# One Trainium2 core, last layer: sixteen shared tiles before the slots, returned rows added at the end, the last router begun inside the attention

## The chip, the cores and the metric

The kernel runs on one of the eight cores of one Trainium2 chip (trn2). A core has TensorE (PE), VectorE (DVE), ScalarE (ACT), GpSimd (POOL) and a queue engine SyncE (SP), each with its own instruction stream; they meet only at semaphores. The metric is the device time of one execution in microseconds; lower is better.

## What is computed

The input `x` is 16 sequences of 128 rows of 256 float32. Four layers follow one another; each adds a gated attention and a gated feed-forward step to `x`. Only the last of each is touched by the change:

```python
x = x + tanh(g_xattn[3]) * L3_xattn(layernorm(x), ctx)   # 16 heads, keys from ctx
x = x + tanh(g_ffn[3]) * L3_ffn(layernorm(x))
# L3_ffn: 7 routed experts of which each row takes 2, and one shared expert for all
gate = xt @ Wr + br                     # 7 logits a row
_, ids = top_k(gate + gate_bias, 2)
probs = softmax(gate where chosen, else -inf)
u = xt @ Wup[e] + bup[e]
g = silu(u @ Wgate[e] + bgate[e]) * u
out = sum_e probs[e] * (g @ Wdown[e] + bdown[e])
out = out + shared expert of the same form, unweighted
```

## The kernel before

`x` stays in on-chip memory as 16 tiles `x[:, t, :]` of 128 rows by 256. All order is written out by hand, one program for each engine; every engine works strictly in the order of its own program. The names that matter:

**The third attention in the code, `attention(3)`.** It runs over the tiles t = 0..15. TensorE computes the scores (`scores(t, c, u)`, two halves c, L1766) into PSUM banks 0 to 3, DVE takes row maxima (L1225) and subtracts them (L1231), ACT exponentiates (L836) with the factor `q_rms`, TensorE turns the result round (`turn`, L1776), ACT copies it out (L842), TensorE multiplies by the values (`values`, L1787) and ACT copies the result (L853). TensorE turns the rows (`turn_rows`, L1799), DVE divides (`denominators`, `norm`, L1238 and L1245), TensorE turns once more (`turn_out`, L1805), ACT copies (`o_evac`, L847), and TensorE applies the output projection (`project_out`, L1811); DVE adds it to `x` (`add_out`, L1133, semaphore `resid6`) and takes mean and variance of the tile (`tile_stats`, L1125 and L1129). POOL makes the reciprocal root from the variance (`deviations(7)`, L584 and L587). The last tile has nothing after it that could fill the waits of this chain. At the front of this attention DVE scales the sums of squares of the queries (`q_var`, L1616), POOL takes the power -1/2 of it (`q_rms`, L803), and only then ACT can exponentiate.

**The router, `router(7, ...)`.** For each tile DVE writes the normalised rows into `xs3` (`norm_rows`, L1529, in the trace as `late`, since that is the buffer), TensorE turns them (`turn_x`, L2048), ACT copies the result into `xt_all` (`route_in`, L989), and TensorE multiplies by the router's weights, 7 columns (L2056). `turn_x` for tile t+2 follows the logits of tile t. After each four tiles DVE chooses two experts per row (`choose`, from L1652 on to L1488), TensorE counts with triangular matrices which place each row gets in its expert (`slots`, L2030 to L2034), and DVE reads that (`place`, L1499 to L1503).

**Sending.** POOL scatters the rows to their places in HBM with indirect DMAs, 32 of them, 128 rows each (`send`, L605), in eight groups of four with a small copy ahead of each (L601). Then SP loads the places back in blocks of 128 rows, called slots (38 of them, `N3`, into a ring of six tiles, L550).

**The expert loop.** The work list is `work3(i)`, i = 0..53: before, i = 0..11 are shared-expert tiles 0 to 11 (`NS3 = 12`), i = 12..49 the 38 slots, i = 50..53 the shared tiles 12 to 15. Each item is a chain: TensorE up and gate in one fused product (`up3`, L2208), DVE adds the bias (`sums`, L1625), ACT Silu (L1089), DVE product (`hidden`, L1631), TensorE turns (`turn_h`, L2216), ACT copies (L1094), TensorE down (`down3`, L2230). TensorE's program for step i is: turn slot i+1 (`turn_slot`, L2091), up of i, down of i-2, turn of i-1. The result of a shared tile is added to `x` (`add_shared`, L1641); that of a slot gets its bias (`out_slot`, L1637) and POOL scatters it to `y_rows` in HBM (`send_back`, L646).

**The end.** SP waits for all scatters, loads the rows back in token order (`yc`, eight loads of 512 KB, L560, four groups `g` of four tiles), and DVE adds them with their weights (`returned(g)`, eight instructions for each group, L1686). Before, `returned(0)` stands in DVE's program at i = 52, ahead of the sums of item 53, and groups 1 to 3 after the loop. SP stores each group of `x` when it is finished (L563).

## Time and profile before

| | us |
|---|---|
| median of 3 runs (lowest, highest) | 897.07 (896.79, 898.49) |
| the profiled execution's own time | 894.69 |
| its span, first to last instruction | 892.9 |

The profile is of one execution. Busy shares over the whole span: PE 84%, DVE 66%, ACT 46%, POOL 40%. The mean granted TensorE clock is 0.915 of full speed. The time outside the span is 894.69 - 892.9 = 1.8 us. In a timeline a row is one instruction or a run of the same one; the bracket at its end is how long the engine was idle before it and what ended that. "x8" counts instructions as the chip ran them (a float32 matmul is two).

### The profile page before, as it was taken

The numbers are of one execution on the slowest core, as the hardware profiler recorded it, in microseconds if no ns is written. First come the engines' busy times: TensorE is split into PE (matmuls) and PEld (weight loads), VectorE is DVE, ScalarE is ACT, GpSimd is POOL, SyncE is SP. The second block draws the span as 40 slices with busy tenths as digits, with TensorE's granted clock in tenths as the row PEclk, the third lists the DMA queues.
The fourth block names the chain that finished last, engine by engine and source line by source line (L and its number), as shares of the span: only waits on it lengthen the run. The fifth ranks groups of instructions, "written<-read, shape, count | busy, mean of one in ns | idle before, by whom it ended". The sixth has DMA issues, their size and how long they took to land.

```text
span 892.9 us, 15919 instructions
## 1 busy us (share of the span) xinstructions
PE 754.0 (84%) x4531; PEld 499.4 (56%) x4539; DVE 586.8 (66%) x1356; ACT 415.2 (46%) x904; POOL 354.8 (40%) x588
## 2 busy tenths in 40 slices
PE   3999795998774289899999968999988889999982
PEld 2455453554342156686888657566657556666651
DVE  5799697677775967873322375788865765445446
ACT  3466465676572014331477554666762132333320
POOL 5000453355447633347377564111131761343320
PEclk9999898999998579959999989999995899999995
DMA  6354308999206891144455352000003222222226
GB/s 209 121 163 144 98 12 274 308 292 313 60 0 252 327 303 45 69 169 159 132 154 155 107 191 76 21 20 21 12 17 132 97 88 80 86 87 86 66 85 213
DMA packets 90652, 117.00 MB, mean 131 GB/s; under 512 B 12438, under 2 KB 81209, under 8 KB 89291
## 3 DMA queue, kind: packets, MB, share of 16 engines
q1 hardware_dynamic: 83802, 99.15, 36.7%
q0 software_dynamic: 6768, 16.86, 5.3%
q8 instruction: 40, 0.66, 0.3%
q14 instruction: 42, 0.34, 0.1%
HBM read 55.04 MB, written 58.43 MB: 127 GB/s over the span
## 4 chain that ended last, share of the span: by engine, by line
PE 50%; DVE 12%; SPq 9%; POOL 9%; issue 9%; ACT 7%; DMA 3%; DVEq 0%; POOLq 0%; ACTq 0%
PE ps L2208 8%; SPq L401 7%; POOL x_rows L605 6%; PE ps L1776 4%; PE ps L2230 4%; PE ps L2098 4%; PE ps L1766 3%; ACT work L836 2%; ACT probs_t L842 2%; PE ps L1973 2%; PE ps L2116 2%; PE ps L1811 2%; PE ps L2091 2%; PE ps L2173 2%; PE ps L1864 2%
## 5 line engine op out<-in xcount | busy, mean ns | idle before, releaser
L842 ACT ACTIVATE probs_t<-ps 128x1024 f32<-128x1024 f32 x64 | 65.5, 1024 | 68.8 <-PE ps L1776 68.8
L1225 DVE TENSOR_REDUCE row_max<-ps 128x8 f32<-128x1024 f32 x64 | 77.5, 1211 | 12.1 <-PE ps L1766 11.8
L1089 ACT ACTIVATE ctx_cols<-ctx_cols 128x256 f32<-128x256 f32 x54 | 22.5, 417 | 123.9 <-DVE ctx_cols L1625 123.9
L1625 DVE TENSOR_TENSOR ctx_cols<-ps,ctx_rows 128x512 f32<-128x512 f32 x54 | 37.3, 691 | 62.3 <-PE ps L2208 62.2
L1231 DVE TENSOR_TENSOR work<-ps,row_max 128x1024 f32<-128x1024 f32 x64 | 76.9, 1202 | 1.2
L1776 PE MATMUL ps<-ident,work 128*128 128x128 f32 x512 | 70.7, 282 | 3.8 <-ACT work L836 2.7
L2208 PE MATMUL ps<-early,xt 128*128 x152 | 71.5, 593 | 0.0
L646 POOL DMA_INDIRECT y_rows<-ctx_cols,w2d x38 | 37.6, 990 | 78.5 <-DMA y_rows<-ctx_cols,w2d 47.1
L2230 PE MATMUL ps<-early,ctx_cols 128*128 (+1 forms) x216 | 57.9, 392 | 11.8 <-ACT ctx_cols L1094 11.8
L1776 PEld LDWEIGHTS ps<-ident,work 128*128 128x128 f32 x512 | 57.3, 143 | 18.4 <-ACT work L836 13.2
L2230 PEld LDWEIGHTS ps<-early,ctx_cols 128*128 128x128 f32 x216 | 41.9, 196 | 41.3 <-issue 23.7
L1787 PEld LDWEIGHTS ps<-probs_t,work 128*32 128x32 f32 x1024 | 24.3, 110 | 52.0 <-ACT probs_t L842 46.7
L587 POOL TENSOR_TENSOR rstd<-var_eps,consts 128x2 f32<-128x2 f32 (+1 forms) x64 | 47.4, 740 | 10.2 <-POOL var_eps L584 5.4
L646 POOL DMA_INDIRECT y_rows<-wgb,probs_t x39 | 38.3, 983 | 22.2 <-issue 16.0
L1787 PE MATMUL ps<-probs_t,work 128*32 128x128 f32 x1024 | 41.7, 281 | 5.4 <-ACT probs_t L842 5.4
L1544 DVE SCALAR_TENSOR_TENSOR xn<-ps,work,xn 128x128 f32<-128x128 f32 x39 | 13.7, 351 | 48.6 <-ACT xn L1021 48.6
L584 POOL TENSOR_TENSOR var_eps<-mv,consts 128x2 f32<-128x2 f32 x64 | 15.0, 235 | 72.6 <-DVE xn L1117 33.2
L2098 PE MATMUL ps<-late,xt 128*128 x156 | 40.1, 380 | 0.0
L669 POOL COPY work<-ctx_rows 128x256 f32<-128x256 f32 x16 | 6.3, 398 | 84.0 <-PE ps L1787 84.0
L1125 DVE BATCH_NORM_STATS2 st<-x 128x6 f32<-128x256 f32 x96 | 35.8, 415 | 4.9 <-POOL x L737 0.9
L1766 PE MATMUL ps<-early,xt_all 64*128 64x512 f32 x128 | 38.5, 679 | 0.0
L1766 PE MATMUL ps<-late,xt_all 64*128 64x512 f32 x128 | 36.7, 651 | 1.9 <-DVE work L1231 1.9
(326 smaller groups left out, 1887.5 us busy)
## 6 DMA issues: line engine op xcount, KB each, us to landing
x_rows<-pad_row SPq DMA_DIRECT2D x1, 17415.0 KB, 68.5
work<-x_rows SPq DMA_DIRECT2D x77, 129.0 KB, 2.1
x_rows<-pad_row SPq DMA_DIRECT2D x1, 7740.0 KB, 35.8
x_rows<-pad_row SPq DMA_DIRECT2D x1, 7611.0 KB, 94.1
early<-in_w3st SPq DMA_DIRECT2D x8, 512.0 KB, 6.4
work<-y_rows SPq DMA_DIRECT2D x16, 256.0 KB, 3.0
early<-y_rows SPq DMA_DIRECT2D x8, 512.0 KB, 7.4
late<-in_w2u SPq DMA_DIRECT2D x1, 2304.0 KB, 8.5
```

The source lines that it names most:

```text
L401: sp.dma_start(kz[HD * h:HD * (h + 1), t % KR, :, h % 4, :], ctx_cols[HD * h:HD * (h + 1), t, :, :]).then_inc(sem(f"att.k{t % KR}"), 16)
L605: pool.indirect_dma_start(out=rows, out_offset=bass.IndirectOffsetOnAxis(ap=pos[:, k, t:t + 1], axis=0), in_=xs[:, t, :], in_offset=None). ...
L646: pool.indirect_dma_start(out=rows, out_offset=bass.IndirectOffsetOnAxis(ap=dest[:, i % 8:i % 8 + 1], axis=0), in_=y[:, i % 4, :], in_offs ...
L842: act.activation(probs_t[:, :, :], ps[:, 4:6, :], ACT.Copy).then_inc(sem("att.evac"), 1)
L1225: dve.tensor_reduce(row_max[:, u, 8 * c:8 * c + 8], scores(c), AX.X, ALU.max).then_inc(sem("att.max"), 1)
L1231: dve.tensor_tensor(probs[:, u, c, :].rearrange("p (h k) -> p h k", k=P), scores(c), row_max[:, u, 8 * c:8 * c + 8].unsqueeze(2).to_broadc ...
L1766: op = mm(bank(2 * c + b), cols(xt_all, t)[64 * b:64 * b + 64, c, :], kz[64 * b:64 * b + 64, t % KR, c, :, :].rearrange("p h k -> p (h k)" ...
L1776: op = pe.transpose(ps[:, 4 + k // 4, (k % 4) * P:(k % 4 + 1) * P], probs[:, u, c, k * P:(k + 1) * P], ident[:, :])
L1787: op = mm(ps[32 * g:32 * g + HV, 6, (2 * c + b) * P:(2 * c + b + 1) * P], vaug[:, u, 8 * c + k, :], probs_t[:, b, g * P:(g + 1) * P], star ...
L2098: op = mm(bank(i % 2, 2 * HID), xti[:, j, :], w2u[:, j, e].rearrange("p w n -> p (w n)"), start=(j == 0), stop=(j == 1))
L2208: op = mm(bank(i % 2), xti[:, j, :], w13[:, e, j, :], start=(j == 0), stop=(j == 1))
L2230: op = mm(bank(4 + i % 2, D), ht3[:, i % 2, j, :], wd3[:, e, j, :], start=(j == 0), stop=(j == 1))
```

## The change

Five edits, all at the last layer:

- `NS3` goes from 12 to 16: all shared tiles stand ahead of the 38 slots, none behind.
- `returned(0)` leaves the loop; all four groups are added after it.
- The router of the last layer is split. TensorE turns tiles 0 and 1 after its last `turn` of the attention, and does the logits of tiles 0 to 7 (`last_logits`, two tiles at a time, each with the turn of the tile two further) at four places between the last tile's steps. Tiles 8 to 15 follow after the attention, with the same `slots` calls, each later by a few tiles. Turned tiles go through banks 2 and 3 instead of 6 and 7, and the logits of the last two groups into banks 6 and 7 (`LB3`), because banks 0 to 3 are free once the scores are.
- DVE normalises rows 0 to 3 and 4 to 11 inside the attention's end, and chooses the experts of group 0 (`choose_last(0)`) ahead of the last `add_out`; the setup of `run3` stands ahead of the attention. POOL makes the roots of tiles 0 to 11 between its steps of the attention (`dev7`).
- At the attention's front DVE does the first row maxima and the first subtraction ahead of `q_var` (`query_variance`), not behind it.

The core of the diff. Left out: the definition of `LB2, LB3`, the same renaming for the router of the layer before (`router` and `route_in` are opened up there with the order unchanged), and `norm_rows` with tile bounds instead of a group number.

```diff
@@ -32,7 +32,7 @@
 RING = 6
-NS3 = 12
+NS3 = 16
 XW = D + 2
...
@@ -804,6 +806,7 @@
             pool.wait_ge(sem("load.w3x"), 16 * 3)
+            dev7 = deviation(7)
             TT(bo_rows, bo_rows, tg[:, 3:4].to_broadcast([P, D]), ALU.mult).then_inc(sem("qk.gain"), 1)
...
                     TT(x[:, t + u, :], x[:, t + u, :], bo_rows, ALU.add).then_inc(sem("out3.bias"), 1)
-            deviations(7)
+                if t >= 4:
+                    dev7(t - 4, t == 4, False)
+            dev7(NT - 4, False, False)
+            dev7(NT - 2, False, False)
@@ -826,6 +832,11 @@
+            def row_out(L, t):
+                act.wait_ge(sem("front.tr"), FRONT[L] + t + 1)
+                act.activation(cols(xt_all, t), bank((TP if L == 5 else 2) + t % 2, D).rearrange("p (j n) -> p j n", j=2),
+                               ACT.Copy).then_inc(sem("front.out"), 1)
...
@@ -865,12 +876,20 @@
                             act.activation(kdec[:, 1:2], kdec[:, 0:1], ACT.Exp, scale=-1.0).then_inc(sem("dec.exp"), 1)
+                        if A == 3 and last and u:
+                            row_out(7, 0)
+                            row_out(7, 1)
                         if A == 3 and before:
...
                     body(t0, t0 == 0, t0 == NT - 2)
+                if A == 3:
+                    row_out(7, 2)
+                    row_out(7, 3)
                 cols_evac(NT - 1)
                 if A == 3:
+                    for t in range(4, 8):
+                        row_out(7, t)
                     o_evac(NT - 1)
@@ -1072,7 +1086,8 @@
-            route_in(7, lambda g: None)
+            for t in range(8, NT):
+                row_out(7, t)
             for i in range(NT + N3 + 2):
...
@@ -1259,10 +1285,12 @@
                     dve.wait_ge(sem("front.tr"), NT)
-                else:
-                    upto(dve, "qkv.mean", 1)
                 row_maxima(0, 0, 0)
+                if A == 3:
+                    upto(dve, "qkv.sum", NT - 4)
                 subtract(0, 0, 0)
+                if A == 3:
+                    query_variance()
...
@@ -1284,15 +1312,22 @@
                             decay_step(t)
+                        elif last and u:
+                            dve.wait_ge(sem("att.scored"), 2 * NC * NT)
+                            norm_rows(7, xs3, 0, 4)
                     if not first:
...
                     body(t0, t0 == 0, t0 == NT - 2)
+                if A == 3:
+                    norm_rows(7, xs3, 4, 12)
                 add_out(NT - 2, 0)
...
                 norm(NT - 1, 1)
+                if A == 3:
+                    choose_last(0)
                 add_out(NT - 1, 1)
...
@@ -1612,13 +1639,22 @@
                 query_squares(t)
-            upto(dve, "qkv.sum", NT)
-            dve.tensor_scalar(q_var[:, :], bank(4, NT), HD / D, HD * RMS_EPS, ALU.mult, ALU.add).then_inc(sem("qkv.mean"), 1)
+            upto(dve, "m2.down", NT + N2)
+            seq(dve.tensor_copy(run3[:, 0], e16[:, 0:E3]))
+            dve.wait_ge(sem("load.w2"), 16 * 5)
+            brb = br3[:, 0:1, :].to_broadcast([P, 4, E3])
+            gbb = br3[:, 1:2, :].to_broadcast([P, 4, E3])
+            def choose_last(g):
+                q = slice(4 * g, 4 * g + 4)
+                dve.wait_ge(sem("main7"), 4 * g + 4)
+                dve.tensor_tensor(lg3[:, q, :], bank(LB3[g], 4 * E3).rearrange("p (t e) -> p t e", t=4), brb, ALU.add
+                                  ).then_inc(sem("rt3.gate"), 1)
+                dve.wait_ge(sem("rt3.gate"), g + 1)
+                seq(dve.tensor_tensor(p3[:, q, :], lg3[:, q, :], gbb, ALU.add))
+                choose(3, E3, g, p3[:, q, :], rt3, cnt3, m3, oh3, run3, red3)
...
-            dve.wait_ge(sem("att.scored"), 2 * NC * NT)
-            for g in range(3):
-                norm_rows(7, xs3, g)
...
@@ -1641,22 +1677,11 @@
-            upto(dve, "m2.down", NT + N2)
-            seq(dve.tensor_copy(run3[:, 0], e16[:, 0:E3]))
-            dve.wait_ge(sem("load.w2"), 16 * 5)
-            brb = br3[:, 0:1, :].to_broadcast([P, 4, E3])
-            gbb = br3[:, 1:2, :].to_broadcast([P, 4, E3])
-            for g in range(NG):
-                q = slice(4 * g, 4 * g + 4)
-                dve.wait_ge(sem("main7"), 4 * g + 4)
-                dve.tensor_tensor(lg3[:, q, :], bank(g, 4 * E3).rearrange("p (t e) -> p t e", t=4), brb, ALU.add
-                                  ).then_inc(sem("rt3.gate"), 1)
-                dve.wait_ge(sem("rt3.gate"), g + 1)
-                seq(dve.tensor_tensor(p3[:, q, :], lg3[:, q, :], gbb, ALU.add))
-                choose(3, E3, g, p3[:, q, :], rt3, cnt3, m3, oh3, run3, red3)
+            place(3, E3, 0, oh3, prod3, posf3, pos3)
+            norm_rows(7, xs3, 12, NT)
+            for g in range(1, NG):
+                choose_last(g)
                 place(3, E3, g, oh3, prod3, posf3, pos3)
-                if g == 0:
-                    norm_rows(7, xs3, NG - 1)
             dve.wait_ge(sem("b3.shared"), 32)
@@ -1708,8 +1733,6 @@
                     hidden(i)
-                if i == NT + N3 - 2:
-                    returned(0)
                 if i == 10:
...
@@ -1719,7 +1742,7 @@
                         seq(dve.tensor_reduce(wk[k], wprod3[k], AX.X, ALU.add))
-            for g in range(1, NG):
+            for g in range(NG):
                 returned(g)
@@ -1833,14 +1856,23 @@
                     turn(t, 1, u)
+                    if A == 3 and t == NT - 1:
+                        pe.wait_ge(sem("att.subbed"), 2 * NC * NT)
+                        turn_x(7, xs3, 0)
+                        turn_x(7, xs3, 1)
                     if A == 3 and t:
                         turn_out(t - 1, 1 - u)
+                if A == 3:
+                    last_logits(0, 2)
                 values(NT - 1, 1, 1)
...
                     project_out(NT - 2)
+                    last_logits(2, 4)
                 turn_rows(NT - 1)
                 if A == 3:
+                    last_logits(4, 6)
                     turn_out(NT - 1, 1)
+                    last_logits(6, 8)
                     project_out(NT - 1)
@@ -2039,28 +2071,28 @@
-            def router(L, E, wr, xs, m, run):
-                def turn_x(t):
-                    pe.wait_ge(sem("xn"), L * NT + t + 1)
-                    if t >= 2:
-                        pe.wait_ge(sem("front.out"), FRONT[L] + t - 1)
-                    for j in range(2):
-                        op = pe.transpose(ps[:, TP + t % 2, j * P:(j + 1) * P], xs[:, t, 2 + j * P:2 + (j + 1) * P], ident[:, :])
-                    op.then_inc(sem("front.tr"), 1)
-                turn_x(0)
-                turn_x(1)
-                for t in range(NT):
-                    pe.wait_ge(sem("front.out"), FRONT[L] + t + 1)
-                    for j in range(2):
-                        op = mm(ps[:, t // 4, (t % 4) * E:(t % 4 + 1) * E], cols(xt_all, t)[:, j, :], wr[:, j, :], start=(j == 0),
-                                stop=(j == 1))
-                    op.then_inc(sem(f"main{L}"), 1)
-                    if t + 2 < NT:
-                        turn_x(t + 2)
-                    if t % 4 == 3 and t > 4:
-                        slots(2 if L == 5 else 3, E, t // 4 - 1, m, run)
-                pe.wait_ge(sem("front.out"), FRONT[L] + NT)
+            def turn_x(L, xs, t):
+                pe.wait_ge(sem("xn"), L * NT + t + 1)
+                if t >= 2:
+                    pe.wait_ge(sem("front.out"), FRONT[L] + t - 1)
+                for j in range(2):
+                    op = pe.transpose(ps[:, (TP if L == 5 else 2) + t % 2, j * P:(j + 1) * P], xs[:, t, 2 + j * P:2 + (j + 1) * P],
+                                      ident[:, :])
+                op.then_inc(sem("front.tr"), 1)
+            def logits(L, E, wr, xs, t):
+                pe.wait_ge(sem("front.out"), FRONT[L] + t + 1)
+                b = (LB2 if L == 5 else LB3)[t // 4]
+                for j in range(2):
+                    op = mm(ps[:, b, (t % 4) * E:(t % 4 + 1) * E], cols(xt_all, t)[:, j, :], wr[:, j, :], start=(j == 0),
+                            stop=(j == 1))
+                op.then_inc(sem(f"main{L}"), 1)
+                if t + 2 < NT:
+                    turn_x(L, xs, t + 2)
+            def last_logits(t0, t1):
+                for t in range(t0, t1):
+                    logits(7, E3, wr3, xs3, t)
...
@@ -2196,7 +2234,13 @@
             pe.wait_ge(sem("resid6"), NT)
-            router(7, E3, wr3, xs3, m3, run3)
+            slots(3, E3, 0, m3, run3)
+            for t in range(8, NT):
+                logits(7, E3, wr3, xs3, t)
+                if t == 13:
+                    slots(3, E3, 1, m3, run3)
+            slots(3, E3, 2, m3, run3)
+            pe.wait_ge(sem("front.out"), FRONT[7] + NT)
```

TensorE at the end of `attention(3)`, before, from the last `turn` (L1776) into the router. `ident,o_n` is `turn_out`, `probs_t,work` `values`, `mid,o_t` `project_out`, `ident,xt` `turn_rows`, `ident,late` `turn_x`, `wr,xt_all` the logits.

```order
L1776 MATMUL ps<-ident,work 128x128 x8
L1805 MATMUL ps<-ident,o_n 128x128 x2
L1787 MATMUL ps<-probs_t,work 32x128 x8
L1811 MATMUL ps<-mid,o_t 128x256 x2
L1799 MATMUL ps<-ident,xt 128x128 x4
L1805 MATMUL ps<-ident,o_n 128x128 x2
L1811 MATMUL ps<-mid,o_t 128x256 x2
L2048 MATMUL ps<-ident,late 128x128 x4
L2056 MATMUL ps<-wr,xt_all 128x7 x2
L2048 MATMUL ps<-ident,late 128x128 x2
L2056 MATMUL ps<-wr,xt_all 128x7 x2
```

The same place after, from the same `turn` on (L1799 now; L2079 is `turn_x`, L2087 the logits, L1810 `values`, L1834 `project_out`):

```order
L1799 MATMUL ps<-ident,work 128x128 x8
L2079 MATMUL ps<-ident,late 128x128 x4
L1828 MATMUL ps<-ident,o_n 128x128 x2
L2087 MATMUL ps<-wr,xt_all 128x7 x2
L2079 MATMUL ps<-ident,late 128x128 x2
L2087 MATMUL ps<-wr,xt_all 128x7 x2
L2079 MATMUL ps<-ident,late 128x128 x2
L1810 MATMUL ps<-probs_t,work 32x128 x8
L1834 MATMUL ps<-mid,o_t 128x256 x2
L2087 MATMUL ps<-wr,xt_all 128x7 x2
L2079 MATMUL ps<-ident,late 128x128 x2
L2087 MATMUL ps<-wr,xt_all 128x7 x2
```

Between the last `turn` and the last `values` there now stand two turns of rows, `turn_out` of tile 14, and the logits of tiles 0 and 1 with two more turns; four such rows of logits and turns stand again ahead of `turn_rows`, ahead of `turn_out` and ahead of the last `project_out`.

DVE at the same place, before: from the last but one tile's division to the router's first sum.

```order
L1245 TENSOR_TENSOR o_n<-ps,rsum 128x256
L1125 BN_STATS st<-x 128x6 x2
L1129 BN_AGGR mv<-st 128x2 x2
L1133 SCALAR_TENSOR_TENSOR x<-ps,tg,x 128x256
L1238 RECIPROCAL rsum<-ps 128x16
L1245 TENSOR_TENSOR o_n<-ps,rsum 128x256
L1133 SCALAR_TENSOR_TENSOR x<-ps,tg,x 128x256
L1125 BN_STATS st<-x 128x6 x2
L1129 BN_AGGR mv<-st 128x2 x2
L1529 TENSOR_SCALAR late<-x,mv,rstd 128x256 x12
L1645 CAST w2d<-moe_c 128x7
L1652 TENSOR_TENSOR work<-ps,br 128x28
```

And after:

```order
L1271 TENSOR_TENSOR o_n<-ps,rsum 128x256
L1231 TENSOR_SCALAR late<-x,mv,rstd 128x256 x4
L1140 BN_STATS st<-x 128x6 x2
L1144 BN_AGGR mv<-st 128x2 x2
L1231 TENSOR_SCALAR late<-x,mv,rstd 128x256 x8
L1148 SCALAR_TENSOR_TENSOR x<-ps,tg,x 128x256
L1264 RECIPROCAL rsum<-ps 128x16
L1271 TENSOR_TENSOR o_n<-ps,rsum 128x256
L1651 TENSOR_TENSOR work<-ps,br 128x28
L1654 TENSOR_TENSOR work<-work,br 128x28
L1508 TENSOR_TENSOR w2d<-work 128x196
L1509 TENSOR_TENSOR w2d<-w2d,lower 128x196
```

The normalised rows 0 to 11 (L1231 now, L1529 before) moved up past `add_out` of tiles 14 and 15, and the choice of group 0 stands between the last division and the last `add_out`; its `place` comes after.

DVE at the very end of the program, before (`ctx_cols<-ps,ctx_rows` is `sums`, `x<-early,w2d,x` is `returned`):

```order
L1625 TENSOR_TENSOR ctx_cols<-ps,ctx_rows 128x512
L1707 TENSOR_TENSOR x<-x,work 128x1024
L1641 SCALAR_TENSOR_TENSOR x<-ps,tg,x 128x256
L1631 TENSOR_TENSOR ctx_cols<-ctx_cols 128x256
L1686 SCALAR_TENSOR_TENSOR x<-early,w2d,x 128x256 x8
L1625 TENSOR_TENSOR ctx_cols<-ps,ctx_rows 128x512
L1641 SCALAR_TENSOR_TENSOR x<-ps,tg,x 128x256
L1631 TENSOR_TENSOR ctx_cols<-ctx_cols 128x256
L1641 SCALAR_TENSOR_TENSOR x<-ps,tg,x 128x256 x2
L1686 SCALAR_TENSOR_TENSOR x<-early,w2d,x 128x256 x24
```

And after:

```order
L1661 ISA
L1661 TENSOR_TENSOR ctx_cols<-ps,ctx_rows 128x512
L1673 ISA
L1673 TENSOR_TENSOR ctx_cols<-ps,work 128x256
L1667 TENSOR_TENSOR ctx_cols<-ctx_cols 128x256
L1673 ISA
L1673 TENSOR_TENSOR ctx_cols<-ps,work 128x256
L1673 ISA
L1673 TENSOR_TENSOR ctx_cols<-ps,work 128x256
L1711 SCALAR_TENSOR_TENSOR x<-early,w2d,x 128x256 x32
```

The loop now ends in results of slots, and the 32 additions of returned rows stand in one piece.

## Rows read from the trace of the kernel before

**Rows 1.** The page: the chain that ended last, shares of the span.

```profile
PE 50%; DVE 12%; SPq 9%; POOL 9%; issue 9%; ACT 7%; DMA 3%; DVEq 0%; POOLq 0%; ACTq 0%
```

**Rows 2.** Windows: length, busy PE, PEld, DVE, ACT, POOL, then clock, DMA.

```profile
668.00:672.00 4.00, 2.52 (x26) 1.46 (x18) 1.16 (x3) 0.61 (x2) 0.00 (x0) 1.00 0.73 220
672.00:676.00 4.00, 2.11 (x5) 1.17 (x4) 1.24 (x3) 0.38 (x1) 0.00 (x0) 0.54 1.05 394
...
692.00:696.00 4.00, 4.00 (x26) 3.94 (x25) 3.41 (x15) 1.30 (x4) 3.19 (x4) 0.50 0.28 99
```

**Rows 3.** Timeline of PE, end of the attention and start of the router.

```profile
667.79 0.64 PE L1787 MATMUL ps<-probs_t,work 128*32 128x128 f32 x16 [0.90 <-ACT probs_t L842]
668.36 1.13 PE L1811 MATMUL ps<-mid,o_t 128*128 128x256 f32 x4
...
672.51 2.07 PE L1811 MATMUL ps<-mid,o_t 128*128 128x256 f32 x4 [0.47 <-ACT o_t L847]
676.85 1.09 PE L2048 MATMUL ps<-ident,late 128*128 128x128 f32 x4 [2.27 <-DVE late L1529]
```

**Rows 4.** Timeline of DVE: last add_out, normalised rows, choose of group 0.

```profile
674.62 0.48 DVE L1133 SCALAR_TENSOR_TENSOR x<-ps,tg,x 128x256 f32<-128x256 f32 x1 [3.08 <-PE ps L1811]
...
676.31 3.95 DVE L1529 TENSOR_SCALAR late<-x,mv,rstd 128x256 f32<-128x256 f32 x12
...
682.66 0.19 DVE L1652 TENSOR_TENSOR work<-ps,br 128x28 f32<-128x28 f32 x1 [2.32 <-PE ps L2056]
...
684.84 0.19 DVE L1483 TENSOR_TENSOR w2d<-w2d,moe_c 128x28 bf16<-128x28 f32 x1
```

**Rows 5.** Timeline of PE: router of the layer before, two neighbouring steps.

```profile
378.08 0.61 PE L2056 MATMUL ps<-wr,xt_all 128*128 128x8 f32 x4 [0.21 <-ACT xt_all L989]
...
378.80 0.85 PE L2056 MATMUL ps<-wr,xt_all 128*128 128x8 f32 x4
```

**Rows 6.** Timeline of PE: this router, two turns, and its end.

```profile
680.03 0.67 PE L2048 MATMUL ps<-ident,late 128*128 128x128 f32 x2
...
681.20 0.67 PE L2048 MATMUL ps<-ident,late 128*128 128x128 f32 x2
...
696.91 3.33 PE L2208 MATMUL ps<-early,xt_all 128*128 128x512 f32 x4
```

**Rows 7.** Timeline of POOL: last root, first and last send.

```profile
676.89 0.81 POOL L587 TENSOR_TENSOR rstd<-var_eps,consts 128x2 f32<-128x2 f32 x1
...
689.56 1.09 POOL L605 DMA_INDIRECT x_rows<-late,w2d  x1 [0.55 <-POOL late L601]
...
731.70 0.96 POOL L605 DMA_INDIRECT x_rows<-late,w2d  x1 [0.30 <-issue]
```

**Rows 8.** Timeline of PE: the first slot's turn.

```profile
737.82 0.41 PE L2091 MATMUL ps<-ident,work 128*128 128x128 f32 x2 [2.09 <-DMA work<-x_rows]
```

**Rows 9.** Group of DVE in 737 to 865 us: busy, mean ns.

```profile
L1625 DVE TENSOR_TENSOR ctx_cols<-ps,ctx_rows 128x512 f32<-128x512 f32 x42 | 29.0, 692 | 55.9 <-PE ps L2208 55.9
```

**Rows 10.** Timeline of PE: the last two items' ups.

```profile
860.98 1.88 PE L2208 MATMUL ps<-early,xt_all 128*128 128x512 f32 x4
...
863.77 1.88 PE L2208 MATMUL ps<-early,xt_all 128*128 128x512 f32 x4
```

**Rows 11.** Timeline of DVE: last out_slot, returned(0), returned(1) to (3).

```profile
861.08 0.42 DVE L1637 TENSOR_TENSOR ctx_cols<-ps,work 128x256 f32<-128x256 f32 x1 [0.29 <-PE ps L2230]
...
869.96 3.25 DVE L1686 SCALAR_TENSOR_TENSOR x<-early,w2d,x 128x256 f32<-128x256 f32 x8 [4.39 <-DMA early<-y_rows]
...
880.07 9.58 DVE L1686 SCALAR_TENSOR_TENSOR x<-early,w2d,x 128x256 f32<-128x256 f32 x24
```

**Rows 12.** Timeline of SP: the loads of returned rows.

```profile
864.51 7.05 SPq L560 DMA_DIRECT2D early<-y_rows  x8
```

**Rows 13.** Timeline of POOL at the front of the attention: q_rms.

```profile
551.59 2.91 POOL L803 TENSOR_TENSOR q_rms<-q_var,consts 128x16 f32<-128x16 f32 x1 [10.50 <-DVE q_var L1616]
```

**Rows 14.** Timeline of ACT at the same place: the first exponential.

```profile
555.45 1.15 ACT L836 ACTIVATE work<-work,q_rms 128x1024 f32<-128x1024 f32 x1
```

41 lines of the change are left out of this document (23 added, 18 removed).

## The prediction

> **What bounds the kernel now.** I began with the page's chain of work that ended last. TensorE holds half of it, and DVE, POOL, SP's queue and ACT share the rest [rows 1]: no engine binds everywhere, so each place that the change touches has to be read by itself. From here on "the router", "the attention" and "the loop" are those of the last layer, and R is the moment at which the last tile of `x` has its attention added (L1133, end at 674.62 + 0.48 = 675.1 [rows 4]).
>
> The windows show the clock [rows 2]. TensorE is at 2.4 GHz until 672 and busy for 2.5 of 4 us just before that. Then the granted clock falls to 0.5, the 1.2 GHz level. It stays there through the whole router, though TensorE is busy all the time in it (4.00 of 4.00 in 692 to 696).
>
> The timeline of TensorE shows the pauses that the change means to fill [rows 3]: it waits 0.90 for ACT ahead of the last `values` at 667.79, the last projection takes 2.07 for four instructions at the low clock against 1.13 for the one before it, and the router cannot start until 676.85, after 2.27 of idleness.
>
> The router then costs one turn and one pair of logits a tile. At 2.4 GHz this was 378.80 - 378.08 = 0.72 in the layer before [rows 5]; here, at 1.2 GHz, it is 681.20 - 680.03 = 1.17. The first product of the loop starts at 696.91 [rows 6], 21.8 after R.
>
> POOL makes its last root until 677.70, then waits for the places of group 0 and sends from 689.56 to 732.66 [rows 7], 43.1 for 32 sends. Send, landing, SP's load: the first slot is there at 737.8, and TensorE had waited 2.09 for it [rows 8]. So before, the loop's start binds through TensorE, and the slots bind by 2.1 more.
>
> In the loop the chain of one item is short work on each engine in turn, 0.69 for the sums for example [rows 9], and TensorE is what paces it: 2.80 for a shared tile, from the up at 860.98 to the next. The up of item 53, the last, starts at 863.77, call it U [rows 10].
>
> The end is a second chain. The last slot's result is formed at 861.08, call it S. The returned rows of group 0 are added from 869.96, 8.9 after S; then DVE is handed back to the two last shared tiles, and 24 additions run from 880.07 to 889.65, 0.40 apiece [rows 11]. The loads of 4.2 MB begin at 864.51 [rows 12], 3.4 after S. The end of the span, 892.9, is 29.1 after U and 31.8 after S.
>
> **The change part by part.**
>
> *Front of the attention: +0.5.* Before, q_rms ran on POOL from 551.59 for 2.91 us [rows 13], beside DVE's maxima and subtraction, and was done 0.95 before the exponential at 555.45 [rows 14] that needs it. Now DVE does maxima and subtraction first. They can start 1.2 earlier, for they no longer wait for the last sums. But q_var comes behind them, at about 552.9, and q_rms ends at 553.0 + 2.9 = 555.9. The cover of POOL's 2.9 is gone, and the exponential comes 0.5 later. Bounds: 0 if POOL releases its semaphore ahead of the row's end, +1.5 if the short low-clock spell there lasts longer.
>
> *The attention's end: R moves from 675.1 to 681.2.* Eight steps of logits and turn, and two turns ahead of them, now stand in front of R. I walk through TensorE's program. The last turn and turn_out end at 667.79 - 0.90 = 666.9; with two turns more, 667.4. The first logits wait for ACT, which must first finish its own copy, until about 668.05; two steps at 0.72 end at 669.5, so `values` starts 1.7 later than before. Values and projection 14 take 1.6, to 671.1; two steps, to 672.6. Here I let the clock fall, as in the row of before. turn_rows, some 0.9, to 673.5; two steps at 1.17, to 675.8; turn_out 0.45; two steps, to 678.6; the last projection 2.07, to 680.7; the addition, R = 681.2. DVE's earlier rows and its choice of group 0 (3.0) fit into its waits of this stretch. POOL's six earlier roots lie in its pauses of the attention, where it waits for TensorE most of the time.
>
> *The router after R: the loop starts at R + 11.0, before R + 21.8.* Two chains run side by side. TensorE: eight steps at 1.17 are 9.4, with three rounds of `slots` about R + 10.2. DVE: statistics and POOL's root until R + 2.6 (677.70 - 675.1), four normalised rows at 0.33 [rows 4] make R + 3.9, choice of group 1 until R + 6.9, place, which waits for TensorE, until R + 8.4, and the part of choice 2 that `slots(2)` needs, 684.84 + 0.19 - 682.66 = 2.4, until R + 10.8. `slots(2)` stands in TensorE's program ahead of the loop, so the later chain counts: 681.2 + 11.0 = 692.2 against 696.9, a gain of 4.7. DVE's work at the head of the loop is as late after its start as before.
>
> *Four more shared tiles ahead of the slots: -2.1, +0.2.* Sends start at about R + 3.1 and need 48.2 to the first slot (737.8 - 689.56), so R + 51.3. TensorE asks for it at the loop's start + 38.8 (737.8 - 2.1 - 696.9), plus four shared items at 2.80: R + 61. It is ready 10 us early, and the wait of 2.09 is gone. DVE's softmax of the choices at i = 10 used that wait as cover; I charge 0.2 for it.
>
> *The tail: +1.9.* The same 54 items stand in the loop, so U moves as its start does. Behind the last up there is now a full item's chain that nothing follows: sums, Silu, product, turn, copy, down. The up itself takes 1.7, the sums 0.7, the rest of the chain, with the down of item 52 in between and the hand-overs, some 3.7: S = U + 6.1 (before, 861.08 was 2.7 ahead of U). The landing and the loads stay as long, so group 0 is added from S + 8.9. The loads take 12 us in all, 3.0 a group, against eight additions of 0.40, 3.2: DVE is just the slower one, so it ends at S + 8.9 + 12.8 = S + 21.7, and the last store needs its 3.25 as before. The end is S + 24.9 = U + 31.0, against U + 29.1. Moving the shared tiles took away what stood beside 8.9 us of round trip, and gave back DVE's broken-up additions.
>
> *Sum.* +0.5 - 4.7 - 2.1 + 0.2 + 1.9 = -4.2. The profiled execution took 894.69, so 890.5; its time was 2.4 below the median of the three runs. I carry the difference over to the median: 897.07 - 4.2 = 892.9.
>
> **The rivals.**
>
> *The clock stays up longer.* The pauses are filled, so TensorE is less idle in 668 to 672. If the clock holds until about 676, the walk gives R = 679.5, the loop starts 6.4 earlier, and the sum is -5.9 (891.2). If it holds through, the last steps run at 0.72 and the last projection at 1.1: R = 677.9, and the sum is -7.5 (889.6). Against holding through: the router kept TensorE busy for 20 us and its clock did not come back. The Trainium skill's page "TensorE: Matmul & The Clock Gate", section "What's actually happening", says that the default state is throttled and activity releases the throttle; by that rule the filled pauses would keep 2.4 GHz and the time would be that of the second case. The row of 692 to 696, all busy and at 0.5, does not agree for this kind of work.
>
> *The clock falls early,* near 669, since values and projection are pushed out by turns and thin products. Then everything from 669 on is at 1.2 GHz: R = 684.1, the loop starts at 695.1, only 1.8 earlier, and the sum is -1.3 (895.8).
>
> *Slower: the pauses are not pauses.* Each of the four places needs turn, ACT's copy and logits in turn. If they don't overlap there, each place costs another 1 us on top of the early fall: R = 688, the loop starts at 699, 2.1 later than now, and with 0.5 - 2.1 + 0.2 + 1.9 the sum is +2.6 (899.7). The break-even is R = 685.4. For it: ACT is in order and copies other things in between. Against: two banks alternate, and in the layer before the step of 0.72 kept its pace with one copy a tile.
>
> *The first slot is late after all,* so that the move does not do what it says. The margin is 10 us, and each of the 32 sends would have to take 0.3 more; the row of the first one reads 1.09.
>
> **How the numbers follow.** Forecast, with a fall of the clock between 671 and 676: 0.45. Clock up throughout: 0.12. Early fall: 0.25. Slower through the pauses: 0.13. Something else, the late slot among it: 0.05. The likeliest case alone spans 890.5 to 894.5. The range takes in the early fall (895.8) with a microsecond for the phase of the clock at 556 and 717, and on the other side the clock that stays up (889.6), again with one: 888.3 to 897.0. About 0.2%, 1.8 us, is what a measurement of this kernel can tell from no change. The forecast, the clock staying up and a third of the early fall are faster by more: 0.66. Within: most of the early fall and some of the rest, 0.20. Slower: 0.14.
>
> **What the profile would show.** Right: the loop's first up at 690 to 693, no wait ahead of the first slot's turn, S 5.5 to 6.5 us after the start of the last up, 32 additions in one piece within 13.5 us of their start, and `q_rms` ending after the first subtraction's table load. The last addition to `x` in the attention should stand at 679 to 682. Wrong: a wait of TensorE for DVE ahead of the loop beyond R + 12; gaps between the 32 additions, which would mean that the loads are the slower; a first exponential later than 557; a low clock in the loop that lasts longer than the two spells of before.

## The result: 887.65 us, ten below before

Four runs of the changed kernel gave a median of 887.65 us (886.41 to 888.64), beside 897.78 us for four of the kernel before; the ratio is 0.9888, with a 95% interval of 0.9871 to 0.9905. The direction was forecast, the size was not: 892.9 was predicted, and the time lies 0.65 below the range. Of the eight executions of the kernel before that stand beside the b runs below, one took 1241.83 us at a granted clock of 0.575, and no ratio uses it.

The changed kernel's profiled execution took 887.76 us, span 886.0. In the code after the change the lines have moved: turn is L1799, values L1810, turn_rows L1822, turn_out L1828, project_out L1834, scores L1789, turn_x L2079, logits L2087, slots L2062 to L2066, up L2252, down L2274, exp L847, add_out L1148, choose's last input L1518, out_slot L1673, returned L1711.

The windows of the changed kernel, with the columns of [rows 2], show the clock at the end of the attention and in the router:

```profile
668.00:672.00 4.00, 2.87 (x28) 2.58 (x25) 3.85 (x15) 2.40 (x6) 1.03 (x2) 1.00 0.20 63
672.00:676.00 4.00, 4.00 (x45) 3.53 (x45) 1.10 (x4) 1.98 (x5) 0.00 (x0) 1.00 0.83 291
676.00:680.00 4.00, 3.30 (x27) 2.84 (x26) 3.50 (x13) 1.81 (x5) 0.00 (x0) 1.00 1.06 380
680.00:684.00 4.00, 3.93 (x36) 3.66 (x37) 3.52 (x15) 1.53 (x4) 2.13 (x4) 0.95 0.17 58
684.00:688.00 4.00, 3.34 (x20) 2.85 (x19) 3.59 (x15) 2.05 (x3) 3.10 (x4) 0.50 0.30 103
```

In [rows 2] the clock had dropped by 672 to 676; here it stays at the 2.4 GHz level until 683.6, and the engine's busy time in 672 to 676 is 4.00 instead of 2.11. The timeline of TensorE shows what that makes of the steps:

```profile
668.45 1.09 PE L1799 MATMUL ps<-ident,work 128*128 128x128 f32 x8 [0.40 <-ACT work L847]
...
673.91 0.51 PE L2087 MATMUL ps<-wr,xt_all 128*128 128x7 f32 x4
...
674.52 0.51 PE L2087 MATMUL ps<-wr,xt_all 128*128 128x7 f32 x4
...
678.27 1.03 PE L1834 MATMUL ps<-mid,o_t 128*128 128x256 f32 x4
...
689.11 0.21 PE L2062 MATMUL ps<-w2d,tri 128*128 128x28 bf16 x1 [1.54 <-DVE w2d L1518]
...
689.33 5.91 PE L2252 MATMUL ps<-early,xt_all 128*128 128x512 f32 x8
```

A step is 674.52 - 673.91 = 0.61, where [rows 6] had 1.17 and [rows 5] 0.72. The last projection takes 1.03 where [rows 3] had 2.07. The router's end has a new wait of 1.54 for DVE's choice, and the loop starts at 689.33.

At the front the timelines of POOL and ACT answer to [rows 13, 14]:

```profile
554.14 2.91 POOL L805 TENSOR_TENSOR q_rms<-q_var,consts 128x16 f32<-128x16 f32 x1 [12.18 <-DVE q_var L1236]
557.09 1.15 ACT L847 ACTIVATE work<-work,q_rms 128x1024 f32<-128x1024 f32 x1 [1.75 <-POOL q_rms L805]
```

The exponential, which had no wait, now waits 1.75 for POOL. The tail, DVE's last result of a slot and its additions, answers to [rows 11]:

```profile
861.06 0.42 DVE L1673 TENSOR_TENSOR ctx_cols<-ps,work 128x256 f32<-128x256 f32 x1 [1.49 <-PE ps L2274]
869.97 12.75 DVE L1711 SCALAR_TENSOR_TENSOR x<-early,w2d,x 128x256 f32<-128x256 f32 x32 [8.49 <-DMA early<-y_rows]
```

DVE now stands still for 8.49 us. TensorE and ACT are done, POOL ends its last scatter at 863.30, and after that only the loads run.

I shall read every run by the distances between six moments, since single executions differ in what lies ahead of the last layer by more than the parts of the change are worth. Q is the start of the last `query_squares` on DVE, T of the attention's last turn, R the end of the last add_out, L the loop's first up, S the start of the last out_slot; "end" is the span. U, the start of the last up, is used beside them, as in the prediction. All in us:

| kernel | Q | Q to T | T to R | R to L | L to S | S to end | Q to end |
|---|---|---|---|---|---|---|---|
| before | 548.54 | 117.04 | 9.52 | 21.81 | 164.17 | 31.82 | 344.36 |
| changed | 549.52 | 118.93 | 11.49 | 9.39 | 171.73 | 24.94 | 336.48 |

The difference is 7.9 us between Q and the end. The medians differ by 10.1, with 8.5 to 11.6 by the interval. The kernel before, profiled again (a0_before, below), had Q at 550.28, and three kernels whose program up to Q is that of before had it at 549.20, 550.85 and 552.78: the profile shown ahead of the prediction has the earliest Q of the five.

### The profile page after: what moved, and what is told of

Read it like the earlier page. It is cut to its first block, busy times and chain, and to the rows that moved or that the text cites. A ratio compares the mean times of both kernels' runs of the same rounds, so it can differ in the third digit from the quotient of the medians.

```text
span 886.0 us, 15903 instructions
## 1 busy us (share of the span) xinstructions
PE 746.5 (84%) x4539; PEld 491.4 (55%) x4539; DVE 587.8 (66%) x1356; ACT 415.0 (47%) x904; POOL 354.7 (40%) x588
## 4 chain that ended last, share of the span: by engine, by line
PE 49%; DVE 16%; issue 10%; SPq 9%; ACT 7%; POOL 6%; DMA 3%; DVEq 0%; POOLq 0%; ACTq 0%
PE ps L2252 10%; SPq L403 7%; PE ps L2274 5%; PE ps L1799 4%; PE ps L2130 4%; POOL x_rows L607 3%; ACT work L847 2%; PE ps L1789 2%; ACT probs_t L853 2%; PE ps L2005 2%; PE ps L2148 2%; PE ps L2123 2%; PE ps L1834 2%; PE ps L1896 2%; PE ps L1810 1%
## 5 line engine op out<-in xcount | busy, mean ns | idle before, releaser
L1799 PE MATMUL ps<-ident,work 128*128 128x128 f32 x512 | 71.3, 284 | 5.6 <-ACT work L847 4.4
L2252 PE MATMUL ps<-early,xt 128*128 x152 | 71.5, 593 | 0.0
L1799 PEld LDWEIGHTS ps<-ident,work 128*128 128x128 f32 x512 | 57.8, 144 | 20.9 <-ACT work L847 14.1
L2274 PE MATMUL ps<-early,ctx_cols 128*128 (+1 forms) x216 | 55.9, 382 | 5.6 <-ACT ctx_cols L1109 5.6
L2274 PEld LDWEIGHTS ps<-early,ctx_cols 128*128 128x128 f32 x216 | 40.6, 190 | 34.7 <-issue 24.6
L1810 PEld LDWEIGHTS ps<-probs_t,work 128*32 128x32 f32 x1024 | 24.4, 110 | 51.4 <-ACT probs_t L853 46.7
L1810 PE MATMUL ps<-probs_t,work 128*32 128x128 f32 x1024 | 41.8, 281 | 4.5 <-ACT probs_t L853 4.5
L1789 PE MATMUL ps<-early,xt_all 64*128 64x512 f32 x128 | 37.8, 669 | 0.0
L1789 PE MATMUL ps<-late,xt_all 64*128 64x512 f32 x128 | 37.1, 657 | 0.8 <-DVE q_var L1236 0.8
```

The source lines that it names most:

```text
L1789: op = mm(bank(2 * c + b), cols(xt_all, t)[64 * b:64 * b + 64, c, :], kz[64 * b:64 * b + 64, t % KR, c, :, :].rearrange("p h k -> p (h k)" ...
L1799: op = pe.transpose(ps[:, 4 + k // 4, (k % 4) * P:(k % 4 + 1) * P], probs[:, u, c, k * P:(k + 1) * P], ident[:, :])
L1810: op = mm(ps[32 * g:32 * g + HV, 6, (2 * c + b) * P:(2 * c + b + 1) * P], vaug[:, u, 8 * c + k, :], probs_t[:, b, g * P:(g + 1) * P], star ...
L2252: op = mm(bank(i % 2), xti[:, j, :], w13[:, e, j, :], start=(j == 0), stop=(j == 1))
L2274: op = mm(bank(4 + i % 2, D), ht3[:, i % 2, j, :], wd3[:, e, j, :], start=(j == 0), stop=(j == 1))
```

## The experiments

Twelve runs. The median times stand beside the kernel before, run on the same chip in the same turn.

**The kernel before once more.** 

> The kernel before, unchanged, for a second profile of it. If the two earlier profiles stand for their kernels, its span is again 892.9, the router's loop starts at 696.9 and the last turn of the attention at 665.6, each to 0.5 us. If a single profile carries a chance part (the changed kernel was already 0.98 us later at the first score of the last layer, in work that both share), the span may lie anywhere from 892 to 896 and the last turn at 665 to 668, while the distances inside the last layer (last turn to the loop's first up 31.3, loop to last up 166.9, last up to the end 29.1) stay within 0.5 us.

One profile: span 894.6, Q to T 117.17, T to R 9.51, R to L 21.81, Q to end 344.32. The distances agree with those of the first profile to 0.13 us, and to 0.21 from L to S, where the slot's wait is 1.81 instead of 2.09, while Q itself moved by 1.7. So distances tell parts of a microsecond; spans don't.

**The front alone.**

```
-                    upto(dve, "qkv.mean", 1)
                 row_maxima(0, 0, 0)
+                if A == 3:
+                    upto(dve, "qkv.sum", NT - 4)
                 subtract(0, 0, 0)
+                if A == 3:
+                    upto(dve, "qkv.sum", NT)
+                    dve.tensor_scalar(q_var[:, :], bank(4, NT), HD / D, HD * RMS_EPS, ALU.mult, ALU.add).then_inc(sem("qkv.mean"), 1)
...
-            upto(dve, "qkv.sum", NT)
-            dve.tensor_scalar(q_var[:, :], bank(4, NT), HD / D, HD * RMS_EPS, ALU.mult, ALU.add).then_inc(sem("qkv.mean"), 1)
             attention(3)
```

> Before with one part alone: query_variance is put behind row_maxima and subtract in the last attention's first item. Theory: this part costs 1.9 us (first score to last turn of the attention 116.4 before, 118.3 with it), because GpSimd's q_rms now starts later, the first exp waits for it and TensorE's first turns and scores fall back to the low clock; time ratio about 1.002. Rival A (my prediction's term): 0.5 us, ratio 1.0005. Rival B: the 1.9 us come from the router part, whose other matmuls shift the attention, and the front is free or gains; ratio 1.000 or below.

897.27 against 897.83, ratio 1.0 (0.9981 to 1.0019). Q to T 119.03: the 1.9 us are there. But T to R was 8.58, 0.94 less, since the last projection still ran at 2.4 GHz (1.13 instead of 2.07): the granted clock fell 8.5 us after T here, and 6.8 after it in the profile of before, though the program of this stretch is the same. Q to end is 344.85, 0.5 above before. As a sum that is rival A's number, by two parts that it did not name. The time alone separates nothing here.

**The router alone**: the changed kernel with `NS3 = 12`, the old front order, and `returned(0)` back in the loop.

```
-NS3 = 16
+NS3 = 12
...
+                if i == NT + N3 - 2:
+                    returned(0)
...
-            for g in range(NG):
+            for g in range(1, NG):
```

> The changed kernel with its router begun in the attention's pauses, but with the old order in front, 12 shared tiles ahead of the slots and the first returned rows added inside the loop. Theory: the router part is the whole gain of the change at this place, last turn to the loop's first up falls from 31.3 to 20.9 us, of which nothing is given back unless the first slot is not ready: the loop asks for it at 24 items of shared work by 2.8 us after its start, about 3 us before it comes at loop start + 41. So 10.4 - 3 + the old slot wait of 2.1 = 8 to 10 us faster, about 888 us. Rival A (prediction's router term): 4.7 us, clock falls at 672 as before, about 892. Rival B: the gain comes from having no slot wait and no returned(0) in the loop, and this kernel is only 2 to 3 us faster.

887.84 against 897.83, ratio 0.9894 (0.9872 to 0.9916): nearly the whole gain of the change, which excludes rival B and by its interval rival A (0.994) as well. T to L is 21.07, as in the changed kernel. The timeline of TensorE shows two costs that this version keeps:

```profile
731.41 0.66 PE L2125 MATMUL ps<-ident,work 128*128 128x128 f32 x2 [4.26 <-DMA work<-x_rows]
...
870.18 2.08 PE L2276 MATMUL ps<-early,ctx_cols 128*128 128x256 f32 x4 [8.23 <-ACT ctx_cols L1109]
```

Against T the loop's start moved 10.3 ahead and POOL's first send only 9.4 (it is at 682.63). That is 0.9 of the 2.2 by which the slot's wait grows, from 2.09 to 4.26. The way from the first send to the slot's turn takes 0.5 more (48.8), and TensorE asks for the slot 0.8 sooner after L (38.0). And 8.23 us of idleness stand after the last up. The timeline of DVE at that place tells why:

```profile
865.55 3.25 DVE L1711 SCALAR_TENSOR_TENSOR x<-early,w2d,x 128x256 f32<-128x256 f32 x8 [4.77 <-DMA early<-y_rows]
868.72 0.68 DVE L1661 TENSOR_TENSOR ctx_cols<-ps,ctx_rows 128x512 f32<-128x512 f32 x1
```

`returned(0)` stands in DVE's program ahead of the last shared tiles' sums. DVE waits there for the DMA, ACT waits for the sums, TensorE for ACT. The kernel before has this wait too.

Unexpected: Q to T is 118.67 with the old front order.

**The tail alone**: the same three places, the other way round, in the kernel before.

```
-NS3 = 12
+NS3 = 16
...
-                if i == NT + N3 - 2:
-                    returned(0)
...
-            for g in range(1, NG):
+            for g in range(NG):
```

> Before with 16 shared tiles ahead of the slots and all returned rows added at the end, nothing else. Theory: it wins the wait of 2.09 us before the first slot's turn and loses 2.6 us behind the last up (last up to end 29.1 before, 31.7 with it): 0.5 us slower, ratio 1.0006. Rival A (prediction): -2.1 + 1.9, 0.2 us faster. Rival B: the low-clock spell near 717 that is gone in the changed kernel belongs to this part, and it is 2 us faster.

899.46 against 897.83, ratio 1.0015 (0.9999 to 1.003). T to R to L is that of before to 0.01, S comes 172.62 after L and the end 24.91 after S: Q to end is 346.02, 1.7 us above before. By the distances this part of the change costs time; by the medians it is not told from nothing. It costs more than the theory's 0.5, and rival A, 0.2 faster, falls, because the slot's wait of 2.09 was not all won. L to U falls only from 166.87 to 165.83. DVE's softmax of the choices, which that wait had covered, now holds up a down:

```profile
745.58 1.13 PE L2228 MATMUL ps<-early,ctx_cols 128*128 128x256 f32 x4 [0.89 <-ACT ctx_cols L1094]
```

Rival B expected the low-clock spell near 717 to go with this part; it is there, at 721 to 725.

**Filled pauses, nothing else.** In the kernel before, at the last tile of the third attention, each added line for `A == 3` alone:

```
+                pe.wait_ge(sem("att.subbed"), 2 * NC * NT)
+                fill(4)
                 values(NT - 1, 1, 1); project_out(NT - 2)
+                fill(3)
                 turn_rows(NT - 1)
+                fill(3)
                 turn_out(NT - 1, 1)
+                fill(2)
                 project_out(NT - 1)
+                fill(8)
...
+def fill(n):
+    for _ in range(n):
+        mm(bank(0).rearrange("p (h k) -> p h k", h=4), ident_bf[:, :], causal_bf[:, :].unsqueeze(1).to_broadcast([P, 4, P]), start=True, stop=True)
```

> Before, with 20 extra matmuls of 128x512 (a bf16 identity against a bf16 mask) put in TensorE's pauses at the last tile of the third attention, written to PSUM bank 0, whose contents nobody reads there; the router itself is untouched. Theory (the pauses cost the clock, and the clock costs the router): the granted clock stays at 1.00 over the last projection and most of the router, so that a router step takes about 0.7 instead of 1.17 us and the last projection 1.1 instead of 2.1; last turn to the loop's first up falls from 31.3 to 24 to 27 us, and the span relative to the first score falls by 4 to 7 us, ratio about 0.994. Rival A (the gain of the change is overlap alone, the clock follows something else): the steps stay at 1.17 us, last turn to loop 31.3 or more, ratio 1.000 or above. Rival B: the clock holds but DVE's choice and the gathers set the loop's start anyway, so that the loop starts at most 2 us earlier.

892.35 against 898.59, ratio 0.9933 (0.9909 to 0.9956). The same work as before plus 20 matmuls for nothing, and it is faster. The windows of this kernel:

```profile
672.00:676.00 4.00, 3.79 (x18) 1.83 (x16) 1.59 (x4) 0.38 (x1) 0.00 (x0) 1.00 1.03 395
676.00:680.00 4.00, 3.25 (x27) 2.71 (x27) 3.98 (x14) 1.55 (x5) 1.03 (x2) 1.00 0.77 255
680.00:684.00 4.00, 4.00 (x23) 3.91 (x22) 2.84 (x12) 1.41 (x4) 0.00 (x0) 0.53 0.01 2
```

TensorE's timeline shows the last projection and two neighbouring steps of the router before the fall:

```profile
673.32 1.13 PE L1811 MATMUL ps<-mid,o_t 128*128 128x256 f32 x4
...
678.32 0.51 PE L2068 MATMUL ps<-wr,xt_all 128*128 128x7 f32 x4
...
678.96 0.61 PE L2068 MATMUL ps<-wr,xt_all 128*128 128x7 f32 x4
```

The clock holds to the 2.4 GHz level until 680.2, 13.8 us after T instead of 6.8, and then falls in the router's thin steps. T to R is 8.58 and R to L 19.58: 3.2 us won by the clock, short of the 4 to 7 that I expected, since only the first four steps ran fast (0.64 to 0.72), and the others took 1.17. Rival A falls. Rival B allowed 2 us and falls narrowly: the loop starts 3.2 us earlier after T than in before, but 2.2 earlier than in a1_front, where the last projection had kept its speed by itself. Q to end is 340.89, 3.5 below before, while the medians differ by 6.2; what is left of that is not placed.

**The changed kernel with the old front order.**

```
-                row_maxima(0, 0, 0)
-                if A == 3:
-                    upto(dve, "qkv.sum", NT - 4)
-                subtract(0, 0, 0)
                 if A == 3:
+                    upto(dve, "qkv.sum", NT)
                     query_variance()
+                    upto(dve, "qkv.mean", 1)
+                row_maxima(0, 0, 0)
+                subtract(0, 0, 0)
```

> The changed kernel with the old order in front of the third attention: query_variance ahead of row_maxima and subtract. First exp comes 7.0 us after the last query_squares instead of 7.57. Theory now (after the router-only kernel, whose attention took 118.7 us from query_squares to the last turn with the old front order too, against 117.1 in the kernel before): the front order matters only through the length of the low-clock spell after the first exp, so 118.7 again or 117.1, span relative to query_squares 0.2 to 1.9 below the changed kernel's 336.5. Rival (my reading of the two traces before any run): the front order costs 1.9 us by itself and this kernel is 1.9 us faster than the changed one, 885.8.

886.96 against 898.59, ratio 0.9865 (0.9834 to 0.9896). Q to T is 117.24, Q to end 336.02. The two expectations overlap at 117.1, so by itself this run settles nothing; the two runs with a filled front, below, do.

**Twelve shared tiles ahead, all returned rows at the end**: the router-only kernel with `returned(0)` moved.

```
-                if i == NT + N3 - 2:
-                    returned(0)
...
-            for g in range(1, NG):
+            for g in range(NG):
```

> The router-only kernel (12 shared tiles ahead of the slots, old front) with one edit: the first returned rows are added at the end instead of inside the loop. Theory: in that kernel DVE stands before returned(0) for the DMA and holds the sums of the last shared tiles, and TensorE idles 8.2 us behind the last up; with the addition at the end the four shared tiles behind the slots run inside the flight of the returned rows. The wait of 4.3 us for the first slot stays. Result of the last slot to the end 24.9 us or up to 2 more, last-query_squares-to-end about 333 to 334 instead of 338.8: about 5 us faster than the router-only kernel and 3 faster than the changed one, 884 to 885. Rival (the prediction's view that returned rows at the end lengthen the tail by 1.9 us): slower than the router-only kernel by about 2, 890.

883.61 against 898.59, ratio 0.9823 (0.9788 to 0.9859). S to the end 25.56 instead of 31.92, Q to end 334.26 instead of 338.81. The rival, which was my prediction's reading of the tail, has the sign wrong. DVE's timeline, the last shared tile and then the additions, which follow without a pause:

```profile
866.07 0.48 DVE L1677 SCALAR_TENSOR_TENSOR x<-ps,tg,x 128x256 f32<-128x256 f32 x1 [1.34 <-PE ps L2274]
866.47 4.83 DVE L1711 SCALAR_TENSOR_TENSOR x<-early,w2d,x 128x256 f32<-128x256 f32 x12
```

The slot's wait is still there, 4.82.

**Thirteen.** `NS3 = 13`, else the same. 

> As the kernel with 12 tiles and all returned rows at the end, but with 13 shared tiles ahead of the slots. Theory: the first slot is ready about 42.3 us after the loop's start and would be asked for at 38.0 + 2.8 = 40.8, so a wait of about 1.5 us is left; the last slot's result comes at the same time as with 12 and three shared tiles (8.4 us) lie in the 8.5 us flight of the returned rows, so equal to it or up to 1 us faster, about 883 to 885. Rival A: what counts is to have all slots' waits gone, so 16 is best and this one is slower than 887.7. Rival B: no difference to 12 within 0.3 us, because the last slot's result and the flight behind it set the end in both.

882.8 against 898.59, ratio 0.9817 (0.9786 to 0.9849): the fastest of all on its chip, and its interval lies below the changed kernel's 0.9871 to 0.9905. On the same chip its executions took 881.35 to 883.71, those of b2_nofront, which differs by three tiles alone, 885.94 to 887.56. The time does not part it from twelve. In the distances it is clearer: Q to end 329.02. Part of the 5.2 us against twelve is the shorter attention (117.20, not 118.57); L to S is 165.39 instead of 169.05. Behind its wait for the slot the kernel with twelve tiles also runs at the low clock for a while, and the next up shows it:

```profile
730.71 0.66 PE L2123 MATMUL ps<-ident,work 128*128 128x128 f32 x2 [4.82 <-DMA work<-x_rows]
731.16 3.62 PE L2252 MATMUL ps<-early,xt_all 128*128 128x512 f32 x4
```

With thirteen, TensorE's timeline has no wait ahead of the first slot, where I expected one of 1.5 to be left, and that up takes 1.88:

```profile
732.84 0.38 PE L2123 MATMUL ps<-ident,work 128*128 128x128 f32 x2
733.06 1.88 PE L2252 MATMUL ps<-early,xt_all 128*128 128x512 f32 x4
```

DVE's timeline has 2.08 left in the returned rows' flight:

```profile
857.00 0.42 DVE L1673 TENSOR_TENSOR ctx_cols<-ps,work 128x256 f32<-128x256 f32 x1 [0.29 <-PE ps L2274]
...
865.92 12.76 DVE L1711 SCALAR_TENSOR_TENSOR x<-early,w2d,x 128x256 f32<-128x256 f32 x32 [2.08 <-DMA early<-y_rows]
```

**Four more, on two other chips.** For three of them the kernel before took 937.49 us, for the last one, on yet another chip, 943.45. Waits of ACT and DVE that the profile puts down to "remote" add up to 61 us in the profile with fourteen tiles; the profiles up to here show none. I read these four runs by distances that are free of them, or beside a run with stops of the same length. First, `NS3 = 14`:

> As the kernel with 13 shared tiles ahead of the slots and all returned rows at the end, but with 14. Theory: with 13 the first slot is already there when it is asked for (no wait at loop start + 41.2), so the fourteenth tile ahead takes 2.8 us from the cover of the returned rows' flight (two tiles, 5.6 us, lie in 8.5 us of flight) and moves the last slot's result 2.8 us back: last query_squares to the end 329.0 + 2.8 = 331.8, with 24.9 us from the last slot's result to the end again; about 885.5 if the front is alike. Rival: the end is set by TensorE's work, which is the same in both, so no difference.

924.4 against 937.49, ratio 0.9891. L to S 183.11 and S to end 24.94; the kernel with thirteen and a filled front, profiled on the same chip with as long a stop in its loop (L to last up 179.69 against 180.20), had L to S 179.79. So the fourteenth tile moved S by 3.3, 0.5 of it the stop: the 2.8 expected. The end moved with it, from 25.00 to 27.83 after the last up, so the rival of no difference falls.

**The router's steps filled**, with thirteen tiles; `fill` now takes the bank as its first argument:

```
             for t in range(8, NT):
                 logits(7, E3, wr3, xs3, t)
+                fill(0, 2)
                 if t == 13:
                     slots(3, E3, 1, m3, run3)
+            fill(0, 4)
             slots(3, E3, 2, m3, run3)
```

> The kernel with 13 shared tiles, plus two extra bf16 matmuls of 128x512 behind each router step after the attention and four ahead of the third slots: TensorE is busier there, at the price of 2 x 0.22 us per step at 2.4 GHz. They write PSUM bank 0 after its logits are read, and nobody reads them. Theory: the clock falls in the router (at about 683) because TensorE has pauses there; filled, it stays at 2.4 GHz, a step takes 0.62 + 0.44, about the 1.17 it took at 1.2 GHz, and the loop's first up takes 3.9 instead of 6.5 us: last add_out to loop start 9.4 to 9.9 as before, the loop 2 to 3 us shorter. Rival: steps of 128x7 matmuls and transposes do not hold the clock whatever is put between them; it falls all the same, a step then takes 1.17 + 0.9 us, and the loop starts about 5 us later.

910.08 against 937.49, ratio 0.9743 (0.9681 to 0.9805). The windows of this kernel, router and first ups:

```profile
704.00:708.00 4.00, 4.00 (x33) 3.38 (x32) 3.57 (x15) 1.53 (x4) 2.61 (x5) 1.00 0.10 36
708.00:712.00 4.00, 4.00 (x33) 3.00 (x34) 1.96 (x11) 2.05 (x3) 2.46 (x4) 1.00 0.32 114
712.00:716.00 4.00, 2.50 (x12) 1.16 (x11) 3.59 (x15) 0.00 (x0) 2.93 (x4) 1.00 0.18 66
716.00:720.00 4.00, 2.31 (x11) 0.94 (x9) 3.20 (x13) 0.42 (x1) 3.11 (x5) 1.00 0.23 83
```

The clock does not leave the 2.4 GHz level, which refutes the rival. But R to L is 11.11, 1.2 longer than with thirteen alone, because filler and step together take 1.05 us, and L to the last up is 166.01 against 165.29, with a slot's wait of 1.66; the theory's loop, 2 to 3 us shorter, did not come. Q to end is 331.97 against 329.02. By the distances a held clock paid for with TensorE's time brings nothing here: the loop's head waits for DVE's choices anyway (1.50 ahead of the third `slots`). The medians say something else: this ratio is the lowest of all. But this kernel's profile has less "remote" waiting: 30 us in all and 3 in the loop, where the one with fourteen tiles has 61 and 27, and the next kernel, also with thirteen, 47 and 19. Whether the fillers have to do with that, or the four executions were lucky, no run shows.

**The front's pauses filled**, once with the old order and thirteen tiles, once in the changed kernel as it is:

```
                 scores(0, 1, 0)
+                if A == 3: fill(7, 6)
...
                     if t + 1 < NT: scores(t + 1, 0, 1 - u)
+                    if A == 3 and t == 0: fill(7, 5)
```

> The kernel with 13 shared tiles, plus extra bf16 matmuls of 128x512 in the two pauses of TensorE at the front of the third attention (six ahead of the third scores, five ahead of the first turn), into PSUM bank 7, which the first turned rows overwrite. Theory: the attention's length (117.0 to 117.2 us from the last query_squares to the last turn in six profiles, 118.6 to 119.0 in four) hangs on the length of the low-clock spell behind these pauses; filled, the spell is gone and it is 116 us or less. Rival: the spell comes all the same, or the extra work delays the first turn, and it stays at 117.0 or above.

> The changed kernel as it is (new front order, 16 shared tiles ahead), plus the extra bf16 matmuls of 128x512 in the two pauses of TensorE at the front of the third attention, as in the run before (into PSUM bank 7, overwritten by the first turned rows). With the old front order and these matmuls the clock stayed at 2.4 GHz and the attention took 116.3 us from the last query_squares to the last turn. Theory: the new order by itself costs only what the first exp comes later, 7.57 instead of 7.05 us, so 116.8 to 117.0 us here, and the 118.9 and 119.0 us of the two profiles with the new order were this plus a longer low-clock spell; the sum from query_squares to the end is 336.5 - 2.0 = 334.5. Rival: the new order costs 1.9 us through a wait that has nothing to do with the clock, and it is 118.2 us or more.

921.14 against 937.49 (ratio 0.9811, 0.9742 to 0.988), and 934.1 against 943.45 (ratio 0.9897, 0.984 to 0.9954). In both the windows over the first turns read 1.00 throughout. Q to T is 116.32 with the old order and 116.81 with the new: 0.49 apart. The first exponential stands at Q + 7.05 and Q + 7.56, 0.51 apart. The last run's theory holds, and its rival (118.2) falls. With the old order the spell is gone as the theory said, though 116.32 is 0.3 above the 116 that it named. In the last run the first slot's turn comes 71 us after L because of the stops, where the changed kernel has 50, so its 334.5 for Q to end can't be read.

## Why the prediction missed

Step by step, in the distances of the two profiles, the sum was -4.2 and the trace gives -7.9:

| term | predicted | Q-to-end distances |
|---|---|---|
| front of the attention | +0.5 | +1.9 (Q to T) |
| attention's end and router | -4.7 | -10.45 (T to L) |
| shared tiles ahead, wait and softmax | -1.9 | -1.9 (L to U) |
| tail behind the last up | +1.9 | +2.6 (U to end) |

**The step that failed is "Here I let the clock fall, as in the row of before".** I walked TensorE's new program with the old program's clock. Up to the end of projection 14 the walk agrees with the trace to 0.1 us, counted from T. The last two pairs of steps and the last projection were priced at 1.2 GHz, R at 681.2, or T + 15.6; it came at T + 11.5. (In the pair of steps ahead of turn_rows, still priced as fast, a step took 0.61 and not 0.72; that is 0.2 of the difference.) From R the loop was put at + 11.0 by DVE's chain; it came at + 9.4. DVE's placing of group 1 no longer waited for TensorE and ended at R + 6.8, not R + 8.4. Of the 5.75 us that the term was short, 4.1 lie ahead of R and 1.6 behind it.

All nine profiles with the moved steps have R at T + 11.5 to T + 11.7, and in none of them does the clock fall before R: in eight it falls 1.9 to 3.8 after R, in the one with filled router steps not in the router at all. So it was no lucky execution.

The right case was on the list with a chance of 0.12, "if it holds through", at -7.5; it held up to R and 3.7 us beyond. I argued against it from a row in which TensorE was busy 4.00 of 4.00 at half clock. That row showed that a clock that was down did not come back in this router; it said nothing on whether a clock still up stays up. What parts the two is shown by b1_fill: with the pauses filled the clock stayed up 7 us longer, the same router, entered at 2.4 GHz, ran four steps fast before it fell, and the projection ahead of it ran at full speed. The Trainium skill ("TensorE: Matmul & The Clock Gate", section "What's actually happening") has activity releasing the throttle. The filled stretches agree with it, 1.00 where the unfilled ones fall to 0.50. In b1_fill and in the changed kernel the clock fell all the same, at 680.2 and 683.6, in the middle of router steps that had followed one another without a pause since 677.6 and 680.0. Why it fell there was not settled.

How much of the 10.45 is clock and how much is overlap? Filling alone gave 3.2 of it (b1_fill), 0.9 in the last projection and 2.2 behind R. I put the rest, some 7, down to the router's steps being in the pauses: eight of sixteen steps and the choice of group 0 are done by R. This split is an argument and not shown, since no run has the moved steps at the low clock.

The prediction's way of carrying over would have made 897.07 - 7.9 = 889.2 of the measured distances, inside the range. The last 1.5 us to 887.65 belong to what no distance places, below.

**Front, +0.5.** The mechanism and the size were right: 0.49 and 0.51 where no clock spell blurs it. What the profile of the changed kernel shows is the case of the bound, "if the short low-clock spell there lasts longer", but with +1.9 it lies beyond the +1.5. These are windows of before, 11.5 to 13.5 us after its Q, and of the changed kernel, 12.5 to 14.5 after its own:

```profile
560.00:562.00 2.00, 2.00 (x28) 1.44 (x28) 1.68 (x2) 0.82 (x2) 0.00 (x0) 1.00 0.07 16
```

```profile
562.00:564.00 2.00, 2.00 (x22) 1.39 (x21) 1.65 (x2) 0.35 (x1) 0.00 (x0) 0.50 0.07 16
```

Q to T was 117.0 to 117.2 in seven profiles and 118.6 to 119.0 in four, of which two have the old order (and 117.9 in the one with filled router steps, where the first exponential came 0.6 late). It goes with the moment at which the clock is back at 2.4 GHz: Q + 11.2 to Q + 11.5 in the seven, Q + 14.4 to Q + 14.8 in the four, Q + 12.2 in the one. Both profiles with the new order and an unfilled front had the long spell; whether the order makes it likelier stays open.

**The slots.** The wait went, as predicted, and the margin was 9 us, not 10. That the term came out at -1.9 is luck in about half of it. The softmax was charged 0.2 and cost a wait of 0.89; the same part alone (a3_tail) shortened L to U by 1.0, and by 0.8 against the second profile of before. The other 0.9 comes from the clock inside the loop: the changed kernel's execution had no low spell behind its head, where before had one, in which an up took 3.25 instead of 1.88:

```profile
717.39 3.25 PE L2208 MATMUL ps<-early,xt_all 128*128 128x512 f32 x4
```

All other profiles have at least one such spell in the loop, b2_nofront too, whose program from R on is that of the changed kernel. So I put the difference down to the execution and not to the change.

**The tail, +1.9, measured +2.6.** S came 6.8 after U, not 6.1: TensorE waits 0.63 and 0.57 for ACT's copies between the last three downs, which my "some 3.7" for the chain left out. S to end was 24.94, as worked out, and the 32 additions took 12.75 in one piece, as its signs said. But the reading behind the term was incomplete. I saw that four tiles moved away from the round trip cost cover, and that group 0's additions in the middle were "broken up"; I did not ask what stood behind those additions. DVE's wait there held back the last shared tiles, so that part of their cover was wasted already in the kernel before. Moving only the additions gained 4.6 us between Q and the end (router alone against twelve tiles). Moving the tiles beyond thirteen gave it back and more: Q to end is 329.02 with thirteen and 336.02 with sixteen (b2_nofront).

**What the sum does not reach.** Medians differ by 10.1, distances by 7.9. The other 2.2 us lie ahead of Q or in executions that the profiles did not catch: the times of before run from 893.39 to 899.23, and the profiled one of before was 3.1 below the median. Carrying the sum to the median was sound in itself, but my range had about a microsecond of width for it. No run settles these 2 us.

Of the signs of being wrong one showed: the first exponential came at 557.09, later than 557; from Q it came 0.66 later than before, and the rest is the late Q. Of the signs of being right two were missed, the first up at 689.33, ahead of 690 to 693, and S 6.8 after U, beyond 5.5 to 6.5.

## What to carry over

Price moved work at the clock that the new program gives itself: ask of each pause that is filled whether it was the pause that let the clock drop, and give that case a real chance. For work that covers a round trip, look up what the waiting engine has queued behind its wait; work placed as cover is none if the waiting instruction stands ahead of it. And choose the number of covering items by two waits at once: here thirteen tiles ahead end the slot's wait and three behind fill all but 2.08 us of the flight; fourteen and sixteen lose on the one side, twelve on the other.

## What the runs showed of the chip

- Twenty matmuls whose results nobody reads made the program 6 us faster (0.9933). They kept the granted clock at 1.00 over a stretch that had dropped to 0.54; 3.5 us of the gain lie behind Q in the profile.
- A low-clock spell of the same place costs 0.9 us in some executions (117.2 against 116.3) and 2.3 in others (118.6), in kernels whose program up to that place is the same.
- In the last four runs ACT and DVE stopped for up to 13.8 us at a time, "remote" by the profile, while none of the ten profiles taken on other chips shows such a wait.
